# Layernorm statistics moved to an earlier stage, and a residual added by VectorE from PSUM

## The chip, the cores and the metric

The kernel runs on one core of a Trainium2 chip. The time is the device time of one execution in microseconds (us). Engine names are those of the profile: PE is TensorE, PEld its weight load, DVE is VectorE, ACT is ScalarE, POOL is GpSimd, SP is SyncE.

## The reference

x has shape (2, 4096, 256) in fp32. Three layers follow each other, a feed-forward, a memory and a feed-forward once more, each on the layernorm of what is there:

```python
x = x + 0.5 * ffn(layernorm(x))
x = x + memory_layer(layernorm(x))
x = x + 0.5 * ffn(layernorm(x))

def ffn(x):                      # token shift, then a gated square of relu
    x_prev = x shifted by one token
    xr = mu_r * x + (1 - mu_r) * x_prev
    xk = mu_k * x + (1 - mu_k) * x_prev
    return sigmoid(xr @ W_r.T) * (square(relu(xk @ W_k.T)) @ W_v.T)

def memory_layer(x):             # 64 quaternions per token
    keys = x @ Wk.T + bk;  keys = keys / max(norm(keys), 1e-12)
    values = x @ Wv.T + bv
    memory = cumsum(quat_mul(values, keys), axis=1)
    retrieved = quat_mul(memory, quat_conj(keys)) / sqrt(positions)
    return x + (layernorm(retrieved) * ln_g + ln_b) @ Wo.T + bo
```

So the memory stage needs the layernorm of two things: of its input x, and of what was retrieved. Its output is x + n + (...), where n is the layernorm of x, and x + n is the residual.

## The kernel before

The whole of x stays in SBUF, in the tile res. Batch b has NT = 32 tiles of 128 tokens by 256 columns. A feed-forward stage takes CT = 4 tiles in a step, so it has 16 steps (j from 0 to 7, b from 0 to 1). The memory stage takes 2 tiles in a step, so it has 32 steps, numbered s = 2j + b. Each engine has its program written out by hand. Within a step the order of the instructions on an engine is fixed, engines wait for each other by counting semaphores, and an engine also waits by semaphore for its own results. The helper rounds() (L38) runs a body for the first steps, then in a loop, then for the last ones, and has(b, d) tells the body whether the step d places away exists. at(j, b, d) (L52) names that step. Below, (j, b) is such a step.

**A feed-forward step (L362 to L478 on DVE, L1050 to L1119 on PE).** PE makes the transposes of the normalized input (L1062), the keys and the receptance (L1046, three passes of a split product), and the values (L1079). DVE multiplies the values by the gate (gating, L409), forms the difference to the token before (L386), mixes keys and receptance (L394) and squares the keys (L402), and then takes the statistics of a block that is normalized later (stats_of: bn_stats L372, a memset L421, bn_aggr L378). POOL adds the gated values to res (residual, L953) and makes the low parts (L284, L946). ACT copies, applies relu and sigmoid, and normalizes (L704).

**A memory step on DVE (body, L604), in this order:** key_unit writes khat from the keys in PSUM (L561); two bn_stats on res for the step three places ahead (L490); bind (L567, tile xn) and retrieve (L567, tile gating_buffers) form products with khat; two bn_stats on ret, the retrieved tile of the step before (L499); bind of the second tile; four bn_aggr, two for res and two for ret (L515); the halves and the total of the sum of ret (ret_halves and ret_total, L222), with n_var (L524) between them; n_rstd (L530); key_max (L548, tile knorm); retrieve of the second tile; n_gain (L537) and n_shift (L538); key_inverse (L554, tile kinv). One chain of layernorm instructions so serves two layernorms: columns 2 and 3 of the n_ tiles are for res, columns 0 and 1 for ret.

**The other engines in a memory step.** PE (L1202): sum_upto (L1155), sum_after (L1162), transposes (L1129), ret_transposes (L1171), project_keys and project_values (L1135, L1137) and, for the step two places back, output (L1182). ACT (L844): ret_normalize (L812), evict_xT (L793), evict_nT (L825), store_x for the step three places back (L819), add_normalized (L785), key_square (L799), the square root std (L768), key_norm (L805) and normalize for the step three ahead (L776), which waits for n_shift. POOL (L994): ret_sum of the second tile, bind_sum (tiles bhalf and kact), key_sum (tile ksum).

**The residual in the memory stage.** add_normalized turns res into x + n in place. Then output adds that to the product in PSUM by a matmul with the identity matrix, and ACT's store_x copies the sum from PSUM to res. output of a step waits until the store of the step before has emptied the bank (x_done).

```python
                        nc.tensor.matmul(o_bank[:, i, :], ones[:, :], bias3[:, 2 * D:], start=False, stop=False)
                        last = nc.tensor.matmul(o_bank[:, i, :], ident[:, :], t[:, i, :], start=False, stop=True)
```

**The seams.** Between the first feed-forward stage and the memory stage DVE runs first_layernorms(0, 1), the last gating, first_layernorms(1, 3) and first_bind (L654 to L657), and ACT runs first_keys (L827). POOL's last residual of the stage follows the last gating. At the end, first_mix of the second feed-forward stage takes the last layernorm of ret between the two mixes of its keys and those of its receptance (L665). The receptance of that stage uses the PSUM bank of the memory's output, so PE waits there for the last store (L1108).

## Time and profile before

| | |
|---|---|
| median of 3 runs | 753.93 us (753.83 to 755.64) |
| the profiled execution | 753.64 us |
| its span, first to last instruction | 751.9 us |
| mean granted TensorE clock | 0.983 |
| busy: PE, DVE, ACT, POOL | 656.5, 611.3, 418.0, 569.6 us |

In the rows below, a line of a timeline gives the start in us from the beginning of the span, the duration in us, the engine, the line of the kernel, the operation, the output and inputs with their shapes, and how many such instructions were merged (x4). In brackets stands how long the engine was idle before it and what ended that. Two instructions that follow each other on DVE overlap by some 0.1 us, so the distance of their starts tells what one adds. A line of stretches gives for each engine the busy time in the stretch and in parentheses the number of instructions, and then the granted clock of TensorE (1.00 is 2.4 GHz), the share of the DMA engines and the GB/s.

### The profile page before, as it was taken

What the parts mean: (1) busy time and instruction counts of PE and PEld (TensorE: products, weight loads), DVE (VectorE), ACT (ScalarE), POOL (GpSimd) and SP (SyncE); (2) the same over time, 40 slices, a digit from 0 to 9 for tenths busy, and PEclk for the clock granted to TensorE, in tenths of its full rate; (3) what the DMA queues carried; (4) which work ended last, traced back from release to release, by engine and by line L of the source; (5) the groups of instructions that cost most, each with busy time, mean ns of one, the idle gap of its engine ahead of it and who ended that gap; (6) DMA issues with size and microseconds to landing.
All of it is one profiled execution on the core that took longest, in us unless ns stands there. A gap on an engine that the chain in (4) does not pass through costs nothing. (4 is left out here: it accounts for less than half of the span.)

```text
span 751.9 us, 13029 instructions
## 1 busy us (share of the span) xinstructions
PE 656.5 (87%) x3536; PEld 542.1 (72%) x3536; DVE 611.3 (81%) x1378; ACT 418.0 (56%) x743; POOL 569.6 (76%) x879
## 2 busy tenths in 40 slices
PE   2888988999779989988988998898867988988897
PEld 2777878888656667766766676676646878878786
DVE  5868667755679999999999999999976668667744
ACT  4666666664534544554455455445446676666652
POOL 3777778776378888888888888888853877788764
PEclk9999999999988999999999999999979999999999
DMA  7710000000000000000000000000000011011102
GB/s 246 231 57 0 0 0 0 0 1 1 0 0 1 1 0 0 0 0 0 0 0 0 0 0 0 0 0 1 1 1 0 29 57 56 30 54 56 56 29 85
DMA packets 18442, 18.67 MB, mean 25 GB/s; under 512 B 752, under 2 KB 18160, under 8 KB 18416
## 3 DMA queue, kind: packets, MB, share of 16 engines
q1 hardware_dynamic: 18416, 18.36, 7.5%
q8 instruction: 12, 0.20, 0.1%
q14 instruction: 14, 0.11, 0.0%
HBM read 9.97 MB, written 8.39 MB: 24 GB/s over the span
## 5 line engine op out<-in xcount | busy, mean ns | idle before, releaser
L222 POOL TENSOR_TENSOR bhalf<-xn 128x128 f32<-128x128 f32 x256 | 118.3, 493 | 30.4 <-DVE xn L567 30.4
L1135 PE MATMUL bank<-wkv,m_xnT 128*128 128x256 f32 x512 | 135.5, 395 | 5.3 <-DVE khat L561 3.3
L409 DVE TENSOR_TENSOR gating_buffers<-bank,gating_buffers 128x1024 f32<-128x1024 f32 x31 | 38.0, 1225 | 95.8 <-issue 55.0
L1079 PE MATMUL bank<-wffn,kact 128*128 128x256 f32 x512 | 115.8, 379 | 0.0
L1135 PEld LDWEIGHTS bank<-wkv,m_xnT 128*128 128x128 f32 x512 | 92.5, 196 | 25.1 <-issue 4.6
L953 POOL TENSOR_TENSOR res<-res,gating_buffers 128x1024 f32 (+1 forms) x31 | 75.2, 2426 | 39.1 <-DVE gating_buffers L409 39.1
L1079 PEld LDWEIGHTS bank<-wffn,kact 128*128 128x128 f32 x512 | 94.8, 190 | 11.6
L284 POOL TENSOR_TENSOR xk_lo<-xk,xk_hi 128x1024 fp32r<-128x1024 f32 x30 | 71.2, 2372 | 33.4 <-ACT xk_hi L712 33.4
L946 POOL TENSOR_TENSOR xr_lo<-xr,xr_hi 128x1024 fp32r<-128x1024 f32 x32 | 76.0, 2374 | 19.0 <-ACT xr_hi L718 16.8
L567 DVE TENSOR_TENSOR xn<-bank,khat 128x1024 f32<-128x1024 f32 x64 | 77.8, 1216 | 1.4
L567 DVE TENSOR_TENSOR gating_buffers<-bank,khat 128x1024 f32<-128x1024 f32 x64 | 77.6, 1212 | 0.0
L1062 PE MATMUL bank<-ident,xn 128*128 128x128 f32 x256 | 37.2, 292 | 42.3 <-DVE xr L394 30.0
L1046 PE MATMUL bank<-wffn_hi,xr_hi 128*128 128x256 f32 x256 | 71.0, 278 | 0.3 <-ACT res L819 0.3
L724 ACT ACTIVATE relu_k<-bank 128x512 f32<-128x512 f32 x64 | 38.2, 599 | 59.3 <-PE bank L1046 59.3
L1046 PE MATMUL bank<-wffn_hi,xr_lo 128*128 128x256 f32 x256 | 70.9, 277 | 0.0
L1046 PE MATMUL bank<-wffn_lo,xr_hi 128*128 128x256 f32 x256 | 70.8, 277 | 0.0
L222 POOL TENSOR_TENSOR rhalf<-gating_buffers 128x64 f32<-128x64 f32 (+2 forms) x160 | 58.9, 402 | 14.0 <-DVE gating_buffers L567 14.0
L704 ACT ACTIVATE xn<-res,shift,rstd 128x256 f32 (+1 forms) x128 | 66.5, 592 | 5.3 <-POOL shift L941 5.3
L1183 PE MATMUL bank<-wo,normedT 128*128 128x256 f32 x256 | 67.3, 386 | 1.5 <-ACT normedT L825 1.5
L768 ACT ACTIVATE n_std<-n_var 128x4 f32<-128x4 f32 (+1 forms) x36 | 7.4, 205 | 106.4 <-DVE n_var L524 106.3
L1062 PEld LDWEIGHTS bank<-ident,xn 128*128 128x128 f32 x256 | 29.6, 148 | 48.7 <-DVE xr L394 23.4
L776 ACT ACTIVATE m_xn<-res,n_shift,n_rstd 128x256 f32 (+1 forms) x64 | 34.9, 592 | 50.2 <-DVE n_shift L538 50.2
(108 smaller groups left out, 1691.7 us busy)
## 6 DMA issues: line engine op xcount, KB each, us to landing
res<-x SPq DMA_DIRECT2D x16, 512.0 KB, 4.5
out<-res SPq DMA_DIRECT2D x15, 512.0 KB, 2.9
wkv<-w_kv SPq DMA_DIRECT2D x1, 512.0 KB, 8.0
out<-res SPq DMA_DIRECT2D x2, 256.0 KB, 2.1
wffn<-w_k SPq DMA_DIRECT2D x1, 256.0 KB, 3.8
wffn<-w_r SPq DMA_DIRECT2D x1, 256.0 KB, 4.6
wffn<-w_v SPq DMA_DIRECT2D x1, 256.0 KB, 6.0
wo<-w_o SPq DMA_DIRECT2D x1, 256.0 KB, 7.2
```

Of the source, the lines that this page charges most:

```text
L222: last = engine.tensor_tensor(o, a, b, op)
L284: ops.tensor_tensor(xk_lo[:, :, :], xk[:, :, :], xk_hi[:, :, :].bitcast(F32), ALU.subtract).then_inc(e["xklo_done"], 1)
L567: nc.vector.tensor_tensor(dst[:, i, :, :].rearrange("p (a b) n -> p a b n", a=4), of.rearrange("p (a n) -> p a n", n=Q).unsqueeze(2).to_br ...
L704: last = nc.scalar.activation(xn[:, b, i, :], t[:, i, :], ACT.Identity, bias=shift[:, b, i:i + 1], scale=rstd[:, b, i:i + 1])
L724: nc.scalar.activation(relu_k[:, o, :], k_ps[:, o, :], ACT.Relu).then_inc(e["relu_done"], 1)
L946: nc.gpsimd.tensor_tensor(xr_lo[:, :, :], xr[:, :, :], xr_hi[:, :, :].bitcast(F32), ALU.subtract).then_inc(e["xrlo_done"], 1)
L953: nc.gpsimd.tensor_tensor(t, t, gated, ALU.add).then_inc(e["res_done"], 1)
L1046: last = nc.tensor.matmul(out_ap, w(f), v(f), start=k == 0, stop=k == n - 1)
L1062: last = nc.tensor.transpose(xT_ps[:, f, i * P:(i + 1) * P], xn[:, b, i, f * P:(f + 1) * P], ident[:, :])
L1079: last = nc.tensor.matmul(dst[:, i, :], x[:, f, i * P:(i + 1) * P], wffn[:, w, f, :], start=f == 0, stop=f == FC - 1)
L1135: nc.tensor.matmul(dst[:, i, :], m_xnT[:, f, i * P:(i + 1) * P], wkv[:, f, col:col + D], start=f == 0, stop=False)
L1183: nc.tensor.matmul(o_bank[:, i, :], normedT[:, f, i * P:(i + 1) * P], wo[:, f, :], start=f == 0, stop=False)
```

## The change

Two things are changed.

First, the statistics of the memory's input are no longer taken in the memory stage. A new function memory_stats runs at the end of each step of the first feed-forward stage on DVE, on the block whose residual was added last. It waits for that residual, takes four bn_stats, waits for them and writes a memset, takes four bn_aggr, waits for them and copies the eight results into x_moments, a tile that holds the moments of all 64 tiles. Square root, reciprocal, gain and shift are then computed for many tiles at once: for 28 of the 32 tiles of each batch with x_variance(0), x_std_of(0) and x_scales(0), and for the last four with x_variance(1), x_std_of(1) and x_scales(1). DVE runs x_scales(0) after the last gating and x_scales(1) after first_bind. normalize and add_normalized on ACT read x_shift, x_rstd and x_gain, and normalize doesn't wait for scales in each step any more. The chain in the memory stage keeps the two columns for ret, and own_stats gets a memset.

Second, the identity matmul in output and its wait for res_done go away. store_x moves from ACT to DVE, where it adds the PSUM bank to res. It stands between ret_total and n_rstd in the step three places later. At the end, two of the stores stand in last_layernorm and one in last_store, behind first_mix.

```diff
+                def memory_stats(j, b):
+                    s = 2 * j + b
+                    dve.wait_ge(e["res_done"], s + 1)
+                    t = tiles(b * NT + j * CT, CT)
+                    for i in range(CT):
+                        last = nc.vector.bn_stats(x_st[:, i, :], t[:, i, :])
+                    last.then_inc(m["x_st_done"], 1)
+                    dve.wait_ge(m["x_st_done"], s + 1)
+                    nc.vector.memset(spare[:, :], 0.0)
+                    for i in range(CT):
+                        last = nc.vector.bn_aggr(x_mv[:, i, :], x_st[:, i, :])
+                    last.then_inc(m["x_mv_done"], 1)
+                    dve.wait_ge(m["x_mv_done"], s + 1)
+                    nc.vector.tensor_copy(x_moments[:, b, bass.ds(j * CT, CT), :], x_mv[:, :, :]).then_inc(m["x_moments_done"], 1)
...
                         if has(b, 4):
                             stats_of(j + 2, b)
+                        if stage == 0 and has(b, -1):
+                            memory_stats(*at(j, b, -1))
...
+                def x_variance(n, first, end):
+                    dve.wait_ge(m["x_moments_done"], 2 * (end // CT))
+                    nc.vector.tensor_scalar(x_var[:, :, first:end], x_moments[:, :, first:end, 1], LN_EPS, None,
+                                            ALU.add).then_inc(m["x_var_done"], 1)
+                def x_scales(n, first, end):
+                    dve.wait_ge(m["x_std_done"], n + 1)
+                    nc.vector.reciprocal(x_rstd[:, :, first:end], x_std[:, :, first:end]).then_inc(m["x_rstd_done"], 1)
+                    dve.wait_ge(m["x_rstd_done"], n + 1)
+                    nc.vector.tensor_scalar(x_gain[:, :, first:end], x_rstd[:, :, first:end], 1.0, None, ALU.add)
+                    nc.vector.scalar_tensor_tensor(x_shift[:, :, first:end], x_moments[:, :, first:end, 0], -1.0,
+                                                   x_rstd[:, :, first:end], ALU.mult, ALU.mult).then_inc(m["x_scales_done"], 1)
...
+                def store_x(j, b):
+                    s = 2 * j + b
+                    dve.wait_ge(m["O_done"], s + 1)
+                    dve.wait_ge(m["res_done"], s + 1)
+                    t = tiles(b * NT + j * 2, 2)
+                    nc.vector.tensor_tensor(t, o_bank, t, ALU.add).then_inc(m["x_done"], 1)
...
                 def body(j, has, start_last):
                     for b in range(2):
-                        s = 2 * j + b
+                        behind = has(b, -1)
                         if not has(b, 1):
                             start_last()
-                        where = at(j, b, -1) if has(b, -1) else None, at(j, b, 3) if has(b, 3) else None
                         if has(b, 1):
                             key_unit(*at(j, b, 1))
-                        ln_stats_res(s + 3, *where)
-                        if has(b, 1):
                             bind(*at(j, b, 1), 0)
                         retrieve(j, b, 0)
-                        ln_stats_ret(s + 3, *where)
-                        own_stats(s + 3, *where)
+                        if behind:
+                            ln_stats(*at(j, b, -1))
                         if has(b, 1):
                             bind(*at(j, b, 1), 1)
-                        ln_moments(s + 3, *where)
+                        if behind:
+                            own_stats(*at(j, b, -1))
+                            ln_moments(*at(j, b, -1))
                         ret_halves(nc.vector, j, b, 0)
-                        ln_variance(s + 3, *where)
+                        if behind:
+                            ln_variance(*at(j, b, -1))
                         ret_total(nc.vector, j, b, 0)
-                        ln_inverse(s + 3, *where)
+                        if has(b, -3):
+                            store_x(*at(j, b, -3))
+                        if behind:
+                            ln_inverse(*at(j, b, -1))
...
             ffn_steps()
-            first_layernorms(0, 1)
+            x_variance(0, 0, NT - CT)
             last_gating()
-            first_layernorms(1, 3)
+            x_scales(0, 0, NT - CT)
+            memory_stats(NJ - 1, 1)
+            x_variance(1, NT - CT, NT)
             first_bind()
+            x_scales(1, NT - CT, NT)
...
                 def first_keys():
                     load_table(ACT.Sqrt)
-                    std(0, 0, 2, 4)
+                    x_std_of(0, 0, NT - CT)
+                    act.wait_ge(m["x_scales_done"], 1)
                     normalize(0, 0)
...
                         if behind:
                             evict_nT(j - 1, b)
-                        if has(b, -3):
-                            store_x(*at(j, b, -3))
...
                     pe.wait_ge(m["normedT_done"], s + 1)
-                    pe.wait_ge(m["res_done"], s + 1)
-                    t = tiles(b * NT + j * 2, 2)
                     need(pe, m["x_done"], s)
...
-                        nc.tensor.matmul(o_bank[:, i, :], ones[:, :], bias3[:, 2 * D:], start=False, stop=False)
-                        last = nc.tensor.matmul(o_bank[:, i, :], ident[:, :], t[:, i, :], start=False, stop=True)
+                        last = nc.tensor.matmul(o_bank[:, i, :], ones[:, :], bias3[:, 2 * D:], start=False, stop=True)
```

## Rows read from the trace of the kernel before

**Rows 1.** The page's first part, busy us, share and instructions of each engine.
```profile
PE 656.5 (87%) x3536; PEld 542.1 (72%) x3536; DVE 611.3 (81%) x1378; ACT 418.0 (56%) x743; POOL 569.6 (76%) x879
```
**Rows 2.** Stretches: memory steps 0 to 2, then 3 to 29; PE, PEld, DVE, ACT, POOL.
```profile
213.75:246.46 32.71, 26.79 (x116) 19.27 (x114) 31.52 (x71) 12.45 (x27) 26.39 (x59) 0.90 0.00 1
246.46:540.12 293.66, 267.49 (x1350) 206.14 (x1350) 289.99 (x670) 150.60 (x325) 250.02 (x541) 1.00 0.00 0
```
**Rows 3.** Timeline of DVE in one steady memory step.
```profile
409.99 0.69 DVE L561 TENSOR_TENSOR khat<-bank,kinv 128x512 f32<-128x512 f32 x1
410.60 0.74 DVE L490 BATCH_NORM_STATS2 n_st<-res 128x6 f32 x2
411.25 1.21 DVE L567 TENSOR_TENSOR xn<-bank,khat 128x1024 f32<-128x1024 f32 x1
...
415.43 0.37 DVE L515 BATCH_NORM_AGGREGATE n_mv<-n_st 128x2 f32<-128x6 f32 x4
415.71 1.88 DVE L222 TENSOR_TENSOR rhalf<-gating_buffers 128x64 f32<-128x64 f32 x5
...
418.22 0.18 DVE L530 RECIPROCAL n_rstd<-n_std 128x4 f32<-128x4 f32 x1
...
419.74 0.15 DVE L537 TENSOR_SCALAR n_gain<-n_rstd 128x2 f32<-128x2 f32 x1
419.80 0.15 DVE L538 SCALAR_TENSOR_TENSOR n_shift<-n_mv,n_rstd 128x4 f32<-128x4 f32 x1
419.87 0.94 DVE L554 RECIPROCAL kinv<-knorm 128x128 f32<-128x128 f32 x1
```
**Rows 4.** Timeline of DVE in one step of the first feed-forward stage.
```profile
95.63 1.40 DVE L372 BATCH_NORM_STATS2 st<-res 128x6 f32 x4
...
100.41 1.22 DVE L409 TENSOR_TENSOR gating_buffers<-bank,gating_buffers 128x1024 f32<-128x1024 f32 x1 [2.96 <-issue]
```
**Rows 5.** Timeline of several engines from the first seam to memory step 0.
```profile
191.62 0.16 DVE L524 TENSOR_TENSOR n_var<-n_mv,eps 128x2 f32<-128x2 f32 x1
...
195.19 1.09 ACT L776 ACTIVATE m_xn<-res,n_shift,n_rstd 128x256 f32<-128x256 f32 x2 [0.50 <-DVE n_shift L538]
...
196.43 0.63 PE L1129 MATMUL bank<-ident,m_xn 128*128 128x128 f32 x4 [0.95 <-ACT m_xn L776]
...
196.88 2.35 POOL L953 TENSOR_TENSOR res<-res,gating_buffers 128x1024 f32<-128x1024 f32 x1 [6.52 <-DVE gating_buffers L409]
...
197.77 1.47 DVE L524 TENSOR_TENSOR n_var<-n_mv,eps 128x2 f32<-128x2 f32 x1
...
203.52 0.23 DVE L548 TENSOR_SCALAR knorm<-knorm 128x128 f32<-128x128 f32 x1 [1.74 <-ACT knorm L805]
...
205.61 2.04 PE L1135 MATMUL bank<-wkv,m_xnT 128*128 128x256 f32 x4 [3.27 <-DVE khat L561]
...
212.13 0.55 DVE L548 TENSOR_SCALAR knorm<-knorm 128x128 f32<-128x128 f32 x1 [4.28 <-ACT knorm L805]
...
222.22 0.23 DVE L548 TENSOR_SCALAR knorm<-knorm 128x128 f32<-128x128 f32 x1 [0.29 <-ACT knorm L805]
```
**Rows 6.** Timeline of DVE at the second seam, its two differences.
```profile
560.83 1.23 DVE L386 TENSOR_TENSOR diff<-bank,xnT 128x1024 f32<-128x1024 f32 x1 [3.70 <-ACT xnT L695]
...
574.76 1.23 DVE L386 TENSOR_TENSOR diff<-bank,xnT 128x1024 f32<-128x1024 f32 x1 [3.61 <-ACT xnT L695]
```
**Rows 7.** Timeline of DVE in step 30, where no bn_stats on res follow khat.
```profile
540.12 0.69 DVE L561 TENSOR_TENSOR khat<-bank,kinv 128x512 f32<-128x512 f32 x1
540.85 1.22 DVE L567 TENSOR_TENSOR xn<-bank,khat 128x1024 f32<-128x1024 f32 x1
```
**Rows 8.** Timeline of PE in a steady step, output.
```profile
405.73 1.03 PE L1183 MATMUL bank<-wo,normedT 128*128 128x256 f32 x4
...
406.70 0.60 PE L1186 MATMUL bank<-res,ident 128*128 x2
407.14 1.03 PE L1183 MATMUL bank<-wo,normedT 128*128 128x256 f32 x4
```

More of the change, by code:

```diff
@@ L476, in last_blocks @@
                         nc.vector.tensor_tensor(t, t, gated[:, span, :], ALU.add).then_inc(last_done, 1)
-                return stats_of, first_mix, steps, last_gating, last_blocks
+                return stats_of, memory_stats, first_mix, steps, last_gating, last_blocks
             def mem():
-                def ln_stats_res(r, ret_at, res_at):
-                    if res_at is not None:
-                        jj, q = res_at
-                        need(dve, m["res_done"], capped(r - 1))
-                        t = tiles(q * NT + jj * 2, 2)
-                        for i in range(2):
-                            nc.vector.bn_stats(n_st[:, q, 2 + i, :], t[:, i, :]).then_inc(m["st_done"], 1)
@@ new lines, in ln_stats, with ln_moments @@
+                def ln_stats(j, b):
+                    s = 2 * j + b
+                    need(dve, m["normed_done"], s - 1)
+                    for i in range(2):
+                        dve.wait_ge(ret_done[i], s + 1)
+                        nc.vector.bn_stats(n_st[:, b, i, :], ret[:, b, i, :]).then_inc(m["st_done"], 1)
+                def ln_moments(j, b):
+                    s = 2 * j + b
+                    for i in range(2):
+                        last = nc.vector.bn_aggr(n_mv[:, b, i, :], n_st[:, b, i, :])
+                    last.then_inc(m["mv_done"], 1)
@@ L584, in retrieve @@
                     all_products(rprod, b, i, memory[b], rprod_done[i])
-                def first_layernorms(start, end):
-                    dve.wait_ge(ffn_sems[0]["res_done"], B)
-                    for r in range(start, end):
-                        where = None, (r // 2, r % 2)
-                        ln_stats_res(r, *where)
-                        own_stats(r, *where)
-                        ln_all(r, *where)
                 def first_bind():
@@ L627, in body @@
                         retrieve(j, b, 1)
-                        ln_scales(s + 3, *where)
+                        if behind:
+                            ln_scales(*at(j, b, -1))
                         if has(b, 2):
@@ L775, in normalize @@
                     for i in range(2):
-                        last = nc.scalar.activation(m_xn[:, i, :], t[:, i, :], ACT.Identity, bias=n_shift[:, b, 2 + i:3 + i],
-                                                    scale=n_rstd[:, b, 2 + i:3 + i])
+                        last = nc.scalar.activation(m_xn[:, i, :], t[:, i, :], ACT.Identity, bias=x_shift[:, b, bass.ds(j * 2 + i, 1)],
+                                                    scale=x_rstd[:, b, bass.ds(j * 2 + i, 1)])
                     last.then_inc(m["xn_done"], 1)
@@ L784, in add_normalized @@
                     for i in range(2):
-                        last = nc.scalar.activation(t[:, i, :], t[:, i, :], ACT.Identity, bias=n_shift[:, b, 2 + i:3 + i],
-                                                    scale=n_gain[:, b, i:i + 1])
+                        last = nc.scalar.activation(t[:, i, :], t[:, i, :], ACT.Identity, bias=x_shift[:, b, bass.ds(j * 2 + i, 1)],
+                                                    scale=x_gain[:, b, bass.ds(j * 2 + i, 1)])
                     last.then_inc(m["res_done"], 1)
@@ L857, in body @@
                             key_square(j + 1, b)
[L858 removed]
+                        if has(b, -1):
+                            std(*at(j, b, -1))
                         if ahead:
```

136 lines of the change are left out of this document (58 added, 78 removed).

## The prediction

> **What bounds the kernel now.** I read the page first: its busy line names no single bound, PE 87%, DVE 81%, POOL 76% [rows 1]. So I split the span by stage. In the memory stage, from 246.46 to 540.12 us, DVE is busy for 289.99 of 293.66 us, while PE has 267.49, POOL 250.02 and ACT 150.60 [rows 2]: VectorE sets the pace, and a change there is worth its effect on DVE's list of instructions. That stretch holds 27 steps, so a step takes 10.88 us. One step in DVE's timeline [rows 3] begins with khat at 409.99 and ends with kinv at 419.87 + 0.94, with nothing idle. In the first feed-forward stage it is different: DVE sits idle for 2.96 us before each gating [rows 4], because PE still makes the values. What is added there lies beside other work as long as it stays under 2.96 us. Last I read the two seams, where a chain runs through ACT, PE, POOL and DVE in turn [rows 5, 6].
>
> The profiled execution took 753.64 us (span 751.9 and 1.7 around it), the median of the runs is 753.93. I work from 753.64 and take the result as the median; the two differ by 0.04%. Under 0.3%, some 2.3 us, a difference here can't be told from no change.
>
> **The part in the first feed-forward stage.** Per step memory_stats adds four bn_stats, a memset, four bn_aggr and one copy of 8 columns. The same list without the copy is there now: from 95.63 to 97.45 (where the idle time before gating begins, 100.41 - 2.96), 1.82 us [rows 4]. With some 0.2 us for the copy and its wait (the small tensor-scalar operations take 0.15 [rows 3]) that is 2.0 us, from 97.45 to 99.45. The gating comes at 100.41, so 0.9 us is left: cost nothing. If the cover were gone, each 0.1 us over it would cost 1.5 us in 15 steps. The wait for the residual's sum holds nothing, since POOL has finished the block of the step before long since.
>
> **The part in the steady memory step.** Spacings count, not durations, since neighbours overlap.
> - Out goes the pair of bn_stats on res. Now khat to bn_stats to bind takes 411.25 - 409.99 = 1.26 us [rows 3]. But the pair also covered bind's wait for khat's own completion; near the end of the stage, where no such pair runs, khat to bind takes 540.85 - 540.12 = 0.73 [rows 7]. Gain 0.53, not 0.65.
> - Two of four bn_aggr: 415.71 - 415.43 = 0.28 for four [rows 3], so 0.14. n_gain: 419.80 - 419.74 = 0.06 [rows 3].
> - In comes the memset, under 0.07 us (bounds 0 and 0.1; the four bn_aggr are 0.07 each).
> - In comes store_x, 512 columns from PSUM and SBUF. The nearest row is khat, the same size and the same two memories: spacing 410.60 - 409.99 = 0.61, busy 0.69 [rows 3]. Bounds 0.55 and 0.75; I take 0.61.
> - Sum: -0.53 - 0.14 - 0.06 + 0.07 + 0.61 = -0.05 us. I use -0.06 with the rounding of the rows. VectorE gets as much work as it loses. For the 26 steps 3 to 28: -1.6 us.
>
> At the wait for khat the Trainium skill speaks otherwise. "VectorE: DVE Perf Modes", section "The DRAIN you can't avoid", says that the next operation starts only once the pipe is empty and that a semaphore between two operations costs nothing extra. By that, khat to bind would cost 0.61 with or without a wait, and the sum at the end would be 3.1 us lower. The trace disagrees, 0.61 without one against 0.73 with one.
>
> **What goes beside it.** PE loses two ident matmuls a step, each with 407.14 - 406.70 = 0.44 us up to the next matmul [rows 8], so 0.88 us, and ACT loses a copy of 0.6. Neither bounds a step. But output now waits for DVE's store_x of the step before. Counted from khat, store_x starts at 7.65 and ends at 8.34; output, which starts 6.6 after khat now (405.73 against 409.99 less a step of 10.88) [rows 3, 8], is held to 8.4 and, shorter by 0.88, ends at 10.4. Behind it on PE stands sum_upto, ready at 11.0; retrieve wants it at 10.8 + 1.86 = 12.7. Slack 1.7 us, so the new wait costs nothing. The keys of the next step come 0.4 us later on PE, ksq still is there when POOL comes to it. Without that slack each step would grow by what is missing.
>
> **Steps without the pair or without the store.** Steps 0 to 2 take 32.71 us now, 1.2 of them idle on DVE [rows 2]. They lose the statistics and have no store_x; step 0 has no layernorm of ret any more (n_var, n_rstd and the rest are some 0.9 us), and ACT's normalize, which used to wait for n_shift at the end of a step, is free, so knorm is early. I get 9.3, 10.2 and 10.1 us: -3.1. Steps 29 and 30 have no bn_stats on res now, so they just gain store_x and the memset: +1.4. In step 31 the store lies before DVE's idle 3.70 us [rows 6]: nothing.
>
> **The first seam.** This decides. Now the first layernorm of the memory is finished before the last gating, and ACT normalizes at 195.19 [rows 5]. After the change x_scales stands behind the last gating on DVE, which starts when the values are there, at 195.5, and takes 1.2 as each gating does [rows 4]: from 196.7 on a reciprocal of 56 columns (0.5 us, between n_rstd's 0.18 for 4 and kinv's 0.94 for 128 columns [rows 3]), x_gain, x_shift. And just then POOL runs the last residual, 196.88 to 199.23 [rows 5]. n_var, with two SBUF inputs, started at 197.77 in that stretch and took 1.47 us, to 199.24, against 0.16 at 191.62 with POOL at rest [rows 5]. x_shift also has two SBUF tensor inputs, and x_gain is of knorm's kind, which took 0.55 beside POOL's work at 212.13 and 0.23 with POOL at rest at 203.52 [rows 5]. So I let both wait for POOL: scales at 199.5, normalize at 199.55, 4.35 later. Bounds: 197.6 if they aren't held, 199.7 if both are in full.
>
> The Trainium skill has the rule behind this: "SBUF — State Buffer", section "Who interferes with whom", says that DVE and GpSimd share a port pair as an exclusive lock, taken by tensor-scalar operations in the two-port mode and, against a GpSimd operation that reads SBUF, by any DVE operation with two SBUF inputs; the second to issue blocks fully. The row of n_var agrees.
>
> Then PE: it ended its values at 195.48 (0.95 before 196.43) [rows 5] and would idle until 200.8, 5.3 us. After an idle time of 3.27 us it now comes back at half clock: four matmuls take 2.04 us at 205.61 [rows 5] against 1.03 for the four of output in the steady step [rows 8]. So transposes (1.1), eviction (0.6) and keys (4.2) run at 1.2 GHz and the values in part; ACT's order puts evict_xT(0,1) before key_norm, so knorm is there at 210.4 and key_max(0,0) at 210.5, not 203.52: +7.0 us (bounds +2.4 and +8). From there to khat(0,1) the chain is as now, half clock included, but for x_scales(1) before the loop: +0.5.
>
> **The second seam.** PE has three outputs there without ident matmuls, -0.9 each, but each store on DVE adds 0.6 to the chain between key mix and receptance mix. PE's transposes(0,1) come at 570.4, and DVE, after the last store at 570.4 and the moved stats_of, is at its difference at 572.95 where it is at 574.76 now [rows 6]: -1.8 us (bounds -0.8 and -2.8).
>
> **Sum.** 7.0 + 0.5 - 3.1 - 1.6 + 1.4 - 1.8 = +2.4 us, 753.6 + 2.4 = 756.0 us. Its own range is 754.0 to 758.5.
>
> **The rivals.**
> - The steady step grows instead of shrinking by 0.05. The place is key_max, which moves 0.6 us later, from the end of POOL's bhalf into its sums for kact. There it can meet a POOL instruction; held ones took 0.55 against 0.23 [rows 5]. From +0.1 us a step on it decides the sign clearly; at +0.25 a step, 26 steps give +6.5: 756.0 + 1.6 + 6.5, about 764; at 0.1, 760. Against it: key_max at 222.22 stood at the start of such sums and took 0.23 [rows 5]. Chance 0.18.
> - The clock holds at keys(0,1). PE idles 3.1 us before it by my count, against the 3.27 us that preceded the fall at 205.61 [rows 5]. Then 4 keys and bias passes take 2.1 us less: 753.9. Chance 0.17.
> - The residual doesn't hold the scales (x_gain slips in ahead, x_shift isn't blocked as n_var was). Normalize comes at 197.65, 1.9 earlier: 754.1; if the shorter idle keeps PE at full clock too, 2.6 more: 751.5. For it: nothing shows x_shift's kind of operation beside a long POOL instruction. Chance 0.13.
> - A wait for the engine's own result costs nothing here: khat to bind then takes 0.61, each of 26 steps 0.12 less, 3.1 us in all: 752.9. The row of 0.73 [rows 7] speaks against it. Chance 0.05. (The Trainium skill's page on VectorE, named above, has this as its rule.)
> - The change doesn't do what it says: the moved statistics don't leave the bound engine. They do; but the eviction comes to it in their place, which is the forecast itself. The rest, 0.05, is for a memory step that shrinks more than I see (key_max finding POOL at rest, -0.2 a step: 751).
>
> **How the numbers follow.** The forecast has 0.42. Half of its own range lies above 756.2, where slower begins. Slower: 0.21 + 0.18 + 0.01 = 0.40. Faster (under 751.7): the low end of the third rival 0.05, some of the fourth 0.02, the rest 0.05 = 0.12. Same: 0.48. The range reaches from 751.0 to 763.0, so that about 1 in 10 is left out on each side.
>
> **What would show it.** In the first stage gating keeps its spacing of 11.0 us. In the memory stage khat to khat is 10.8 us, DVE still without idle time, khat to bind 0.73, PE idle before output. At the first seam ACT's first m_xn begins near 199.5 right after POOL's residual, PE's first keys take 2 us per four matmuls, key_max(0,0) begins near 210.5. Step 0 is near 9.3 us. If m_xn begins at 197.7, or key_max before 207, the time is lower; if the steady step is over 10.9, or key_max takes 0.4 in it, it is higher.

## The result, and the profile after

The changed kernel takes 759.07 us (median of 5 runs, 758.83 to 760.51) beside 755.64 for the kernel before in the same runs (753.83 to 755.79). The ratio is 1.006, with a 95% interval of 1.0043 to 1.0077: slower by some 4.5 us, where I forecast slower by 2.4. The medians alone lie only 3.4 us apart, since the times of the kernel before fall into two groups (753.83 and 753.93, then 755.64 to 755.79) and its median lies in the upper one. It was timed a second time, with e10_after_again below, and gave 1.0058 (1.0045 to 1.0072). The profiled executions differ by 5.2 us (753.64 and 758.83; spans 751.9 and 757.1), and their difference can be followed row by row.

The first part of the page of the changed kernel: busy us, share, instructions. Against [rows 1] PE lost 23 us and ACT 14, DVE gained 31: PE and ACT were relieved, but the engine that sets the memory stage's pace was not.

```profile
span 757.1 us, 12708 instructions
PE 633.6 (84%) x3408; PEld 527.9 (70%) x3408; DVE 642.7 (85%) x1437; ACT 403.9 (53%) x709; POOL 568.6 (75%) x879
```

The first feed-forward stage: DVE in a step from the middle, then POOL and DVE ahead of the last gating but one. The memory's statistics fit in the middle of the stage: 0.92 us of idle time is left before gating, where I had counted 0.9. Towards the end they don't. The copy of 8 columns takes 0.17 us at 99.74 and 1.79 at 186.16, where it ends together with POOL's xr_lo (185.55 + 2.38 = 187.93).

```profile
99.74 0.17 DVE L444 COPY x_moments<-x_mv 128x8 f32 x1 [0.17 <-DVE x_mv L441]
100.83 1.23 DVE L411 TENSOR_TENSOR gating_buffers<-bank,gating_buffers 128x1024 f32<-128x1024 f32 x1 [0.92 <-PE bank L1086]
...
185.55 2.38 POOL L953 TENSOR_TENSOR xr_lo<-xr,xr_hi 128x1024 fp32r<-128x1024 f32 x1
...
186.16 1.79 DVE L444 COPY x_moments<-x_mv 128x8 f32<-128x8 f32 x1
187.87 1.21 DVE L411 TENSOR_TENSOR gating_buffers<-bank,gating_buffers 128x1024 f32<-128x1024 f32 x1
```

The last line has no idle time before it: this gating was held by the copy. The last gating of the stage comes at 196.65, 1.08 after the 195.57 of before.

The first seam of the changed kernel, several engines (start, duration, and in brackets the idle time and what ended it), against [rows 5]:

```profile
196.65 1.23 DVE L411 TENSOR_TENSOR gating_buffers<-bank,gating_buffers 128x1024 f32<-128x1024 f32 x1 [2.93 <-issue]
197.79 0.49 DVE L509 RECIPROCAL x_rstd<-x_std 128x56 f32<-128x56 f32 x1
197.95 2.34 POOL L960 TENSOR_TENSOR res<-res,gating_buffers 128x1024 f32<-128x1024 f32 x1 [6.39 <-DVE gating_buffers L411]
198.31 2.06 DVE L511 TENSOR_SCALAR x_gain<-x_rstd 128x56 f32<-128x56 f32 x1
...
200.25 0.20 DVE L512 SCALAR_TENSOR_TENSOR x_shift<-x_moments,x_rstd 128x56 f32<-128x56 f32 x1
...
200.50 1.09 ACT L794 ACTIVATE m_xn<-res,x_shift,x_rstd 128x256 f32<-128x256 f32 x2 [5.08 <-DVE x_shift L512]
...
201.73 1.09 PE L1136 MATMUL bank<-ident,m_xn 128*128 128x128 f32 x4 [5.58 <-ACT m_xn L794]
...
203.49 2.08 PE L1142 MATMUL bank<-wkv,m_xnT 128*128 128x256 f32 x4 [0.68 <-ACT m_xnT L811]
...
210.38 0.23 DVE L550 TENSOR_SCALAR knorm<-knorm 128x128 f32<-128x128 f32 x1 [7.78 <-ACT knorm L823]
```

All of the chain that I had drawn is there: the scales behind the last gating, x_gain held until POOL's residual is done (197.95 + 2.34 = 200.29), normalize right after, PE back at half clock (2.08 us for four key matmuls), key_max(0,0) at 210.38.

One steady memory step on DVE, against [rows 3], and PE's output in it, against [rows 8]:

```profile
402.88 0.69 DVE L563 TENSOR_TENSOR khat<-bank,kinv 128x512 f32<-128x512 f32 x1
403.61 1.22 DVE L569 TENSOR_TENSOR xn<-bank,khat 128x1024 f32<-128x1024 f32 x1
...
407.67 0.18 DVE L526 BATCH_NORM_AGGREGATE n_mv<-n_st 128x2 f32<-128x6 f32 x1
...
407.83 2.25 DVE L225 TENSOR_TENSOR rhalf<-gating_buffers 128x64 f32<-128x64 f32 x5
410.00 0.42 DVE L531 TENSOR_TENSOR n_var<-n_mv,eps_pos 128x2 f32<-128x2 f32 x1
410.35 0.41 DVE L225 TENSOR_TENSOR ret<-rhalf 128x256 f32<-128x256 f32 x1
410.68 0.68 DVE L603 TENSOR_TENSOR res<-bank,res 128x512 f32 x1
411.28 0.15 DVE L536 RECIPROCAL n_rstd<-n_std 128x2 f32<-128x2 f32 x1
411.35 0.20 DVE L550 TENSOR_SCALAR knorm<-knorm 128x128 f32<-128x128 f32 x1
```
```profile
411.50 1.10 PE L1188 MATMUL bank<-wo,normedT 128*128 128x256 f32 x4 [1.67 <-DVE res L603]
```

The stages of the changed kernel (window, its length, busy us and instructions of PE, PEld, DVE, ACT, POOL, granted clock): memory steps 0 to 2, steps 3 to 29, then to the first difference of the second feed-forward, to the second, and to the next gating. The first two answer [rows 2].

```profile
220.42:251.04 30.62, 25.59 (x110) 18.74 (x110) 28.94 (x57) 13.23 (x28) 25.53 (x58) 0.89 0.00 1
251.04:543.83 292.79, 241.07 (x1238) 189.31 (x1236) 288.82 (x594) 138.14 (x296) 250.07 (x541) 1.00 0.00 0
543.83:565.71 21.88, 13.09 (x47) 9.76 (x46) 18.01 (x56) 7.01 (x15) 15.35 (x36) 0.75 0.00 0
565.71:578.09 12.38, 10.67 (x52) 8.01 (x51) 10.15 (x27) 7.84 (x13) 2.38 (x1) 0.90 0.01 1
578.09:591.48 13.39, 10.33 (x56) 9.21 (x55) 8.47 (x27) 10.07 (x17) 9.26 (x14) 0.87 0.00 1
```

Before, the last three are 20.71, 13.93 and 11.76 us long. With those landmarks the 5.2 us are split up without a rest:

| Stretch | Forecast | Measured, from rows |
|---|---|---|
| start to key_max(0,0) | +7.0 | +6.86 (203.52, 210.38) |
| to khat(0,1) | +0.5 | -0.19 (213.75, 220.42 stand 6.67 apart) |
| steps 0 to 2 | -3.1 | -2.09 (32.71, 30.62) |
| 26 steady steps | -1.6 | -1.45 (283.46, 282.01) |
| steps 29, 30, to the first difference | +1.4 | +1.75 (30.91, 32.66) |
| between the two differences | -1.8 | -1.55 (13.93, 12.38) |
| to the next gating, and the rest | 0 | +1.63 (11.76, 13.39) and +0.24 |
| sum | +2.4 | +5.2 |

### The profile page after: what moved, and what is told of

Same layout as the page of the kernel before. It is cut to its first block and busy times, and to the rows that moved or that the text cites. A ratio compares the mean times of both kernels' runs of the same rounds, so it can differ in the third digit from the quotient of the medians.

```text
span 757.1 us, 12708 instructions
## 1 busy us (share of the span) xinstructions
PE 633.6 (84%) x3408; PEld 527.9 (70%) x3408; DVE 642.7 (85%) x1437; ACT 403.9 (53%) x709; POOL 568.6 (75%) x879
## 5 line engine op out<-in xcount | busy, mean ns | idle before, releaser
L1188 PE MATMUL bank<-wo,normedT 128*128 128x256 f32 x256 | 70.1, 405 | 50.8 <-DVE res L603 49.5
L1188 PEld LDWEIGHTS bank<-wo,normedT 128*128 128x128 f32 x256 | 45.6, 199 | 69.4 <-issue 60.1
L225 DVE TENSOR_TENSOR rhalf<-gating_buffers 128x64 f32<-128x64 f32 (+2 forms) x160 | 69.2, 494 | 0.0
```

The lines of the kernel that those rows point to most:

```text
L225: last = engine.tensor_tensor(o, a, b, op)
L1188: nc.tensor.matmul(o_bank[:, i, :], normedT[:, f, i * P:(i + 1) * P], wo[:, f, :], start=f == 0, stop=False)
```

## The experiments

Four questions were open. Is the cost really in the first seam, and the two parts worth what I said (e1 to e4)? Why do the halves of ret take longer in the steady step than before (e5)? What holds x_gain, and what do the waits at output cost (e6, e7)? Is it the clock that makes the first keys late (e8, e9, e11)?

Since medians taken at different times differ a little, I compare ratios to the kernel before, and rows by their distance from a landmark. The one that shifts most is the start: in the profiles of e1, e5, e6, e8, e9, e10 and e11 everything from some 35 us on comes 1.4 to 2.1 us later, since PE's granted clock dropped between some 29 and 35 us. The last section has its numbers.

**e1_scales_first**: the changed kernel, x_scales(0) ahead of the last gating.

```diff
-            last_gating()
             x_scales(0, 0, NT - CT)
+            last_gating()
```

> The changed kernel with one edit: x_scales(0) stands ahead of the last gating on DVE instead of behind it. My theory: in the changed kernel DVE's first m_xn release comes at 200.5 us, since x_scales(0) waits behind the last gating and then behind POOL's last residual (x_gain took 2.06 us, to 200.3). Ahead of the gating the square root is there at 195.4, reciprocal 0.5, gain and shift 0.3, so m_xn begins near 196.4 and the gating is late by 0.1 at most. PE's idle time before its first transposes falls from 5.6 us to about 1.5, so they and the first keys run at full clock, and key_max(0,0) moves from 210.4 back to about 205. The time falls by 5 us against the changed kernel, to about that of the kernel before (ratio 0.999). Rival: the seam is bound elsewhere (the statistics of the last block, or the chain of knorm), then key_max(0,0) stays within 1 us of 210.4 and the ratio near 1.006.

Measured: 753.65 us, ratio 0.9981 (0.9966 to 0.9996). The loss is gone, and a little more. In its timeline x_gain takes 0.19 us, since POOL is not at work yet:

```profile
197.55 0.19 DVE L511 TENSOR_SCALAR x_gain<-x_rstd 128x56 f32<-128x56 f32 x1
...
197.81 1.23 DVE L411 TENSOR_TENSOR gating_buffers<-bank,gating_buffers 128x1024 f32<-128x1024 f32 x1
197.90 1.09 ACT L794 ACTIVATE m_xn<-res,x_shift,x_rstd 128x256 f32<-128x256 f32 x2 [0.92 <-DVE x_shift L512]
...
199.14 0.63 PE L1136 MATMUL bank<-ident,m_xn 128*128 128x128 f32 x4 [1.42 <-ACT m_xn L794]
...
207.59 0.23 DVE L550 TENSOR_SCALAR knorm<-knorm 128x128 f32<-128x128 f32 x1 [3.86 <-ACT knorm L823]
```

This profile has the late start (1.60 at the gating of 100.83, which is at 102.43 here), so key_max(0,0) is 4.4 us earlier than in the changed kernel. I had expected the first keys to run at full clock, and that didn't come about: after 1.42 us of idle time they are at half clock too (1.89 us for a group of four), and from the transposes to key_max it still takes 8.45 us (8.65 in the changed kernel). What the moved line gives is the earlier m_xn.

**e2_stats_only**: the changed kernel, with the residual left to TensorE and ScalarE as before. **e3_store_only**: the kernel before, with the residual added by VectorE and nothing else.

The heart of the diff of e2 against the changed kernel (e3 has the same edit the other way round, against the kernel before); store_x also goes back to ACT's program and out of DVE's:

```diff
-                    nc.vector.tensor_tensor(t, o_bank, t, ALU.add).then_inc(m["x_done"], 1)
+                    nc.scalar.copy(tiles(b * NT + j * 2, 2), o_bank).then_inc(m["x_done"], 1)
...
-                        last = nc.tensor.matmul(o_bank[:, i, :], ones[:, :], bias3[:, 2 * D:], start=False, stop=True)
+                        nc.tensor.matmul(o_bank[:, i, :], ones[:, :], bias3[:, 2 * D:], start=False, stop=False)
+                        last = nc.tensor.matmul(o_bank[:, i, :], ident[:, :], t[:, i, :], start=False, stop=True)
```

> The changed kernel with its second part undone: the statistics are taken in the first feed-forward stage as in the change, but the residual is added by the identity matmul on PE and copied out by ACT, as before. My theory: the steady memory step is DVE's list, 10.78 us in the changed kernel, and store_x is 0.60 of it; the step falls to about 10.18 us, 26 steps give 15.6 us, and the time is near 742 us (ratio 0.984). Rival: PE or POOL becomes the bound once DVE's list is shorter (PE had about 9.6 us of work a step with the identity matmul, POOL 9.3): then the step stays over 10.5 us, DVE shows idle time in it, and the time is over 750.

> The kernel before with only the second part of the change: store_x on DVE adds PSUM to res, the identity matmuls are gone, the statistics stay in the memory stage. My theory: store_x adds 0.60 us to each of 29 steady steps, 10.88 to 11.48 us, 17 us in all, less 1.5 at the second seam: near 770 us (ratio 1.021). The first seam is that of the kernel before, key_max(0,0) near 203.5. Rival: taking 0.88 us from PE and 0.6 from ACT gives something back in the step: then the step is 11.2 or less.

Measured: e2 743.21 us, ratio 0.9855 (0.9828 to 0.9881), steady step 10.313 us (250.82 to 518.97 for 26). e3 764.44 us, ratio 1.0133 (1.0115 to 1.0152), steady step 11.241. Against the 10.902 of before the statistics are worth -0.59 and the store costs +0.34 a step; both together give not -0.25 but -0.055 (10.847). So the one part is a clear gain and the other a clear loss, and in the changed kernel they nearly cancel. For e2 I had expected 742 us, for e3 770: the store costs less than its own 0.60 us.

My list had -0.66 for the first and +0.61 for the second. In e3 the store costs only 0.34. Most of what is missing is this: n_rstd and key_max stand behind it and no longer wait, they are followed by the next instruction after 0.08 and 0.12 us there, after 0.20 and 0.18 before. And in e3 PE's wait for the store does something that I had excluded; its output falls to half clock inside steady steps:

```profile
412.60 1.10 PE L1183 MATMUL bank<-wo,normedT 128*128 128x256 f32 x4 [2.15 <-DVE res L609]
...
413.70 1.92 PE L1183 MATMUL bank<-wo,normedT 128*128 128x256 f32 x4
```

**e4_stats_scales_first**: e2 and e1 together.

> Both edits together: statistics in the first feed-forward stage, the residual on PE and ACT as before, and x_scales(0) ahead of the last gating. If the two are independent, it is 5 us under the kernel with the statistics alone, near 737 us (ratio 0.977). If the seam's loss is hidden by something else once the steps are shorter, it is equal to it.

Measured: 738.88 us, ratio 0.9792 (0.9773 to 0.9811). It beats the kernel before by some 16 us and the changed one by some 20. The steady step is 10.317 us as in e2, key_max(0,0) comes at 206.13.

**e5_extra_aggr**: the changed kernel, with work added to the bound engine.

```diff
+                        nc.vector.bn_aggr(x_mv[:, i, :], n_st[:, b, i, :])
                         last = nc.vector.bn_aggr(n_mv[:, b, i, :], n_st[:, b, i, :])
```

> The changed kernel with two more bn_aggr on VectorE in every memory step, ahead of the operation that halves the retrieval's result; their result is not used. They add about 0.14 us of work to each of some 30 steps. Theory A (VectorE waits at the halving for GpSimd's key_sum, whose end sets the time at which the halving ends): the halving starts later and takes that much less, 2.03 us from start to start where the changed kernel has 2.17; the steady step stays at 10.85 us and the kernel within 1 us of the changed kernel. Rival B (VectorE's list is simply a sum): the halving stays at 2.17, the step is 10.99 us and the kernel 4 us longer than the changed kernel, 763 us.

Measured: 760.55 us, ratio 1.0088 (1.007 to 1.0106); by the times alone, neither theory is excluded. The trace decides for A in the steady step. The step is 10.852 us for 10.847, and from the last gating to the one at the second seam it is 394.40 us (198.27 to 592.67), in e10_after_again 394.39. In its timeline the halves begin 5.08 us after khat, where the changed kernel has 4.95, and n_var follows 7.12 us after khat in both:

```profile
404.42 0.69 DVE L564 TENSOR_TENSOR khat<-bank,kinv 128x512 f32<-128x512 f32 x1
...
409.50 2.12 DVE L225 TENSOR_TENSOR rhalf<-gating_buffers 128x64 f32<-128x64 f32 x5
411.54 0.42 DVE L532 TENSOR_TENSOR n_var<-n_mv,eps_pos 128x2 f32<-128x2 f32 x1
```
```profile
409.27 0.72 POOL L990 TENSOR_TENSOR ksum<-ksq 128x256 f32<-128x256 f32 x1
```

POOL's key_sum begins 4.85 us after khat in both (407.73 in the changed kernel), and n_var follows its start by 2.27 us in both. So the end of the halves goes with POOL's key_sum, and 0.13 us more of DVE's work ahead of them costs nothing. The kernel before has the same distance, 2.28 us, though DVE comes to its halves 0.47 us after the start of key_sum and not 0.10 as in the changed kernel:

```profile
415.24 0.73 POOL L982 TENSOR_TENSOR ksum<-ksq 128x256 f32<-128x256 f32 x1
417.52 0.43 DVE L524 TENSOR_TENSOR n_var<-n_mv,eps 128x4 f32<-128x4 f32 x1
```

**e6_residual_dve**: the changed kernel, the last residual of the first feed-forward on VectorE behind x_scales(0), not on POOL.

```diff
             x_scales(0, 0, NT - CT)
+            dve.wait_ge(ffn_sems[0]["gated_done"], NS)
+            last_t = tiles(2 * NT - CT, CT)
+            nc.vector.tensor_tensor(last_t, last_t, gated, ALU.add).then_inc(ffn_sems[0]["res_done"], 1)
...
                     rounds(pool, NJ, 1, 2, body)
-                    if stage == 0:
-                        residual(NJ - 1, 1)
```

> The changed kernel with the last residual addition of FFN0 on VectorE behind x_scales(0), where the changed kernel has it on GpSimd. Theory A (x_gain is held by GpSimd's residual at the shared SBUF port): x_gain takes about 0.2 us, where the changed kernel has 2.06; the first normalized x of the memory (m_xn) starts at about 198.7 us where the changed kernel has 200.5; key_max(0,0) starts some 1.8 us earlier, at about 208.6, if the clock behaves alike, and the kernel is 1 to 2 us faster than the changed kernel. The residual on VectorE lies in the time in which it waits for keys(0,0). Rival B (x_gain is long for another reason, the distance to its own inputs): x_gain stays near 2 us and the first seam and the time don't change.

Measured: 756.67 us, ratio 1.0028 (1.0016 to 1.0041), some 2.3 us under the changed kernel. x_gain takes 0.19 us, and m_xn starts 2.02 us after the last gating (200.24 - 198.22) where it is 3.85 in the changed kernel: the 1.8 us that I had put down to POOL's residual.

```profile
199.89 0.19 DVE L511 TENSOR_SCALAR x_gain<-x_rstd 128x56 f32<-128x56 f32 x1
...
200.12 1.22 DVE L671 TENSOR_TENSOR res<-res,gating_buffers 128x1024 f32<-128x1024 f32 x1
200.24 1.09 ACT L797 ACTIVATE m_xn<-res,x_shift,x_rstd 128x256 f32<-128x256 f32 x2 [3.24 <-DVE x_shift L512]
```

Only 0.76 of it arrives at key_max(0,0) (12.97 after the last gating, 13.73 in the changed kernel), since more of the keys run at half clock in this profile (2.08, 1.92 and 1.75 us for a group of four matmuls; in the changed kernel 2.08, 1.45 and 1.03). Against e10_after_again, where they take 2.08, 1.92 and 1.74, it is 2.0 (14.97 - 12.97).

**e7_early_store**: the changed kernel, store_x ahead of the first retrieve of the step.

```diff
                             bind(*at(j, b, 1), 0)
+                        if has(b, -3):
+                            store_x(*at(j, b, -3))
                         retrieve(j, b, 0)
...
                         ret_total(nc.vector, j, b, 0)
-                        if has(b, -3):
-                            store_x(*at(j, b, -3))
```

> The changed kernel with store_x ahead of the retrieval's first operation of the step, where the changed kernel has it after. Theory A (in the changed kernel store_x covers the waits of n_rstd and knorm for VectorE's own results, and TensorE's wait for PSUM at the output costs nothing): TensorE's idle time ahead of the output falls from 1.67 us to under 0.3, but the steady step grows by 0.1 to 0.2 us, to 10.95 to 11.05, and the kernel by 3 to 5 us over the changed kernel; in the second seam the half clock at the last output goes, worth 0.6 us of that. Rival B (the wait at the output costs): the step is shorter than 10.85 us and the kernel faster than the changed kernel.

Measured: 758.31 us, ratio 1.0054 (1.0035 to 1.0073), not to be told from the changed kernel. The trace shows neither theory as written. PE's output has no idle time before it any more, and the steady step is 0.07 us shorter (10.776), not 0.1 to 0.2 longer. It is not the wait at output: n_rstd and key_max do wait again (spaced 0.20 and 0.14), but the halves, which DVE reaches 5.55 us after khat, take 1.92 us for 2.17. As in e5, they are shorter when they begin later; only here they begin 0.84 us after the start of key_sum, and n_var follows it by 2.76 us, no longer by 2.27. Steps 28 and 29 are 0.24 us longer each, its first seam is longer (15.29 us from the last gating to key_max(0,0), 13.73 in the changed kernel, with three groups of keys at half clock), and a half-clock stretch in the second seam is missing, in this one profile: the second difference to the next gating takes 11.72 us, as before, where it is 13.39 in the changed kernel. I can't say what share of its 10 runs has that.

**e8_pe_filler** and **e9_filler_short**: the changed kernel, with 22 and with 11 matmuls without use while PE waits for the memory's first m_xn. Nothing else differs.

```diff
+                pe.wait_ge(ffn_sems[0]["gate_done"], NS)
+                for _ in range(22):
+                    nc.tensor.matmul(o_bank[:, 0, :], wkv[:, 0, 0:P], wkv[:, 0, 0:D], start=True, stop=True)
```

> The changed kernel with 22 matmuls without use on TensorE between the last values of FFN0 and the first transposes of the memory, into a bank that is overwritten later. They keep TensorE at work where the changed kernel has it idle for some 5 us. Theory A (the granted clock falls to half in that idle time and makes keys(0,0) and keys(0,1) slow, 2.08 us where 1.04 is the time at full clock): the keys run at full clock, key_max(0,0) starts 2 to 3 us earlier than 210.4 us, and the kernel is 1 to 3 us faster than the changed kernel. Rival B (what follows m_xn on ScalarE and VectorE sets the time of key_max(0,0), not the clock): key_max(0,0) stays within 0.5 us of 210.4 and the time doesn't change.

> As e8_pe_filler, with 11 matmuls in place of 22, since those ran for 9.66 us and held the first transposes back by some 3.6 us. The 11 should take 4.8 us and end ahead of the first transposes, which stay 5.1 us behind the last gating. Theory A (the half clock after TensorE's idle time is what makes the first keys late): from the first transposes to key_max(0,0) it is 6.8 us, as in e8_pe_filler, where the changed kernel has 8.65; key_max(0,0) starts 11.9 us after the last gating where the changed kernel has 13.7, and the kernel is 1.9 us faster or more. Rival B (the clock falls all the same, since these matmuls do not count or end too early): 8.6 us or more from the transposes to key_max(0,0), and no gain.

Measured: e8 759.84 us, ratio 1.0074 (1.0058 to 1.0089): no gain. Its filler ran for 9.66 us, longer than the idle time, and held the transposes back to 206.88, 4.98 us behind m_xn instead of 1.23. But the clock behaved as theory A says: 6.74 us from the transposes to key_max(0,0). In e9 the filler fits, and the time follows: 756.35 us, ratio 1.0025 (1.0005 to 1.0045), 2.5 us under e10_after_again. The filler there ends at 202.94, ahead of the transposes at 203.70. The timeline of e9:

```profile
198.03 4.91 PE L1198 MATMUL bank<-wkv 128*128 128x256 f32 x22
...
203.70 0.66 PE L1136 MATMUL bank<-ident,m_xn 128*128 128x128 f32 x4 [0.75 <-ACT m_xn L794]
...
205.03 1.13 PE L1142 MATMUL bank<-wkv,m_xnT 128*128 128x256 f32 x4 [0.68 <-ACT m_xnT L811]
...
210.49 0.23 DVE L550 TENSOR_SCALAR knorm<-knorm 128x128 f32<-128x128 f32 x1 [5.83 <-ACT knorm L823]
...
212.58 2.05 PE L1142 MATMUL bank<-wkv,m_xnT 128*128 128x256 f32 x4 [2.95 <-DVE khat L563]
```

From the transposes to key_max(0,0) it is 6.79 us for 8.65 (9.89 in e10), and 11.80 from the last gating for 13.73 (14.97 in e10). The last line shows what is given back: the half clock now comes at keys(0,1), after 2.95 us of idle time, and khat(0,0) to khat(0,1) takes 9.55 us where it is 8.79 in the changed kernel. It isn't the 2.95 us alone that brings this: e8 has the same idle time there, and its keys(0,1) take 1.10 us.

**e10_after_again**: the changed kernel itself, beside e9 and e11.

> The changed kernel itself, on the same chip and beside the same runs of the kernel before as e9_filler_short and e11_best_filler, to compare them with it directly. The first comparison gave a ratio of 1.006; both theories expect 1.005 to 1.008 here.

Measured: 759.43 us, ratio 1.0058 (1.0045 to 1.0072). Its profile shows how far one execution of the same kernel is from another: from m_xn (201.87) to key_max(0,0) (213.00) it takes 11.13 us, where the first profile has 9.88, since three groups of keys and not two run at less than full clock.

**e11_best_filler**: e4_stats_scales_first with three such matmuls (range(3)).

> e4_stats_scales_first (the statistics moved, the residual left to TensorE and ScalarE, x_scales(0) ahead of the last gating) with three matmuls without use on TensorE ahead of the memory's first transposes. In e4_stats_scales_first TensorE is idle there for 1.42 us, and the first keys run at half clock; from the transposes to key_max(0,0) it is 8.45 us. Theory A (even this short idle time lets the clock fall): with 1.3 us of it filled the clock holds, it is 6.8 us, and the kernel is 1 to 1.7 us faster than e4_stats_scales_first, some 737 us. Rival B (the clock falls for what lies before, not for this idle time): it stays at 8.4 us and the time at 739 us.

Measured: 738.89 us, ratio 0.9787 (0.9774 to 0.98). The mechanism is A's, the time B's. From the transposes (199.01) to key_max(0,0) (205.81) it is 6.80 us for 8.45: with the idle time of 1.42 us filled, the keys behind it run at full clock. But the next keys are at half clock again (2.04 at 207.90), which takes 0.5 us back, and no gain can be measured in the end. In these two profiles 1.25 us of it is there at khat(0,1) (18.24 us behind the last gating for 19.49), and 0.45 is left at the gating behind the second seam (373.79 for 374.24), where the values take 4.90 us in e11 and 3.62 in e4.

```profile
197.51 1.46 PE L1198 MATMUL bank<-wkv 128*128 128x256 f32 x6
...
199.01 0.66 PE L1133 MATMUL bank<-ident,m_xn 128*128 128x128 f32 x4
...
205.81 0.23 DVE L550 TENSOR_SCALAR knorm<-knorm 128x128 f32<-128x128 f32 x1 [1.58 <-ACT knorm L808]
...
207.90 2.04 PE L1139 MATMUL bank<-wkv,m_xnT 128*128 128x256 f32 x4 [2.95 <-DVE khat L563]
```

## Why the prediction was right, and where its sizes were off

The direction and the place were right: the memory stage gives a little back, and the first seam takes more. e1 shows the place; one line moved there is worth 0.8%. The size was too small, 2.4 us for 4.5, and the 759.07 us lie just over the forecast's own range (754.0 to 758.5). That is near where rival one begins (760), but the steady step didn't grow: what was missing is in steps 0 to 2 and behind the second difference, and that the sum came out no further off owes something to errors that cancel.

**First feed-forward, predicted 0, measured +1.08.** The cover was sized rightly (0.92 us left for 0.9), but from a step in the middle of the stage. Some 0.4 of it is there from the first steps on (gating at 34.61 for 34.20, at 100.83 for 100.41). The rest is from the last steps, where the order of the list brings the copy beside POOL's xr_lo, 1.8 us for 0.2: the distance to the kernel before is 0.43 at the gating of 178.09, 1.26 at the next and 1.08 at the last. I used the port rule for the scales and not for the copy, which is in the same change. The Trainium skill names copy among the operations that can take the shared pair ("SBUF — State Buffer", "Who interferes with whom"); the 1.79 agrees. That no copy would cost less wasn't tried.

**The hold of the scales, right.** Normalize was predicted at 199.55, 4.35 later; less the 1.08 it came at 199.42. It was x_gain that POOL held, and e6 confirms the cause. Rival three falls.

**The half clock, right in kind; its size isn't the same in every execution.** From normalize to key_max(0,0) I had 10.95 us. In this profile it took 9.88: I let nearly all keys run at half speed, and the clock was back at some 206. In e10_after_again, the same kernel, it took 11.13. e9 shows that it is the clock: with PE kept at work it is 7.94 us (202.55 to 210.49). So the forecast of 210.5 was met at 210.38 by luck: the stage before ended 1.1 us late, and the half clock of this execution was 1.1 us shorter than mine.

The +6.86 at this seam are 1.08 for the late end of the stage, 1.83 for the hold (m_xn 3.85 us after the last gating, 2.02 in e6), 2.40 for scales that stand behind the gating at all (2.02 after it, where m_xn was 0.38 ahead of it before), and 1.94 for the clock (9.88 for the 7.94 of e9), less 0.39, since at full clock that way took 8.33 before.

**Rival two, the clock holds at keys(0,1): half true, and priced too high.** Its groups take 1.30, 1.92, 1.50 and 1.03 us in the changed kernel and 1.10, 1.03, 1.03 and 1.03 in e10; in the kernel before they take 2.04, 1.91, 1.91 and 1.11. But khat(0,0) to khat(0,1), 8.98 us before (204.77 to 213.75), is 8.79 and 8.46: it gives some 0.5 us, not 2.1. The 0.19 are the whole difference of the table's second line, where I had +0.5.

**Steps 0 to 2, predicted -3.1, measured -2.09.** Step 0 takes 9.87 us for 9.3; key_max waits 1.41 us for ACT in step 1. I summed DVE's list where the chain through the other engines still set the end.

**The steady step, predicted -0.06, measured -0.055, and not as listed.** khat to bind is 0.73 as said, so rival four falls: an own wait costs 0.12 us here. The store takes 0.60. But two entries were missing, and they nearly cancel, which is luck: store_x covers the waits of n_rstd and key_max (0.07 and 0.12 for 0.20 and 0.18), and the halves take 2.17 for 1.81. Their end is tied to the start of POOL's key_sum in both kernels, and that moved up by only 0.40 us (4.85 after khat for 5.25), where DVE's list ahead of them lost 0.77 (4.95 for 5.72). e2 and e3 show the parts, -0.59 and +0.34, and that they don't add up; e5 shows why. Rival one didn't come about at key_max (0.20 us), but something of its kind did, at the halves. What remains of the last rival, a step that shrinks by 0.2, is in neither profile of the changed kernel.

**PE's wait at output, predicted free, is free in the steady step.** It is 1.67 us, and e7, which takes it away, gains 0.07 us, no more than the halves give. At the end of the stage it isn't: PE is idle for 4.01 us before the output at 552.11, falls to half clock, and DVE waits 0.59 us for it at 557.25. That is in the +1.75 for 1.4.

**The second seam, predicted -1.8, measured -1.55; behind it +1.63 that I had not.** There the transposes of the second feed-forward and the values behind them run at half clock in part, 1.85 and 4.55 us; at full clock (e7) they take 1.06 and 3.62:

```profile
585.18 1.85 PE L1069 MATMUL bank<-ident,xn 128*128 128x128 f32 x8 [3.06 <-DVE xr L396]
...
586.82 4.55 PE L1086 MATMUL bank<-wffn,kact 128*128 128x256 f32 x16
```

This is the step of the prediction that failed outright: it ended at the difference, and let all behind it be as before. PE was idle for 2.12 us before those transposes and is for 3.06 now, since it gets through the products ahead of them sooner: it starts them 1.85 us ahead of the difference instead of 1.33, and no longer waits 0.33 us for ACT's copy in them. From the second difference to the next gating it is over 13 us in seven profiles with that gap (after, e1, e5, e6, e8, e9, e10), and 11.75 in e2 and e4, whose gap is 2.02. But e7 has the gap of 3.06 and 11.72, e3 one of 3.20 and 11.72, and e11 has 2.03 and 13.44. So the gap doesn't decide alone. Whether the change brings the half clock there or only some executions have it is open, and of the kernel before there is one profile; I made no experiment there.

## What to carry to other kernels

Work that leaves the bound engine is worth only what isn't put in its place: here the moved statistics gave 11 us and the residual cost 10, and leaving the second part out made 743 us of 759. When work moves across a stage boundary, read the boundary's list in order and ask of each small operation which long instruction of another engine it will stand beside; one line moved ahead of the gating was worth 5 us. And sum a list only between the points where another engine sets the time: ahead of such a point 0.13 us more cost nothing (e5), and of 0.77 us that went 0.40 arrived.

## What the runs showed of the hardware that I had not expected

- The granted clock falls in some executions and not in others of the same kernel. In the first feed-forward it was 1.00 between 30 and 40 us in the changed kernel's first profile, and 0.72 between 30 and 35 in e10_after_again's, of the same kernel, which made all behind it 1.4 us later (last gating at 198.03 for 196.65). What decides wasn't looked for.
- An idle time of PE of no more than 1.42 us, ahead of four short transposes, was followed by half clock on the keys (e1, e4: 1.89 and 1.96 us for four matmuls); with three matmuls in it they took 1.13 (e11), and so they did before, after an idle time of 0.95. Filling it took the half clock from these keys and gave it to the next. The length of an idle time doesn't decide alone: after the same 2.95 us keys(0,1) take 2.05 in e9 and 1.10 in e8 and e10.
- An operation of a few columns is held by POOL about as long as a larger one: the copy of 8 columns took 1.79 us for 0.17, x_gain with 56 columns 2.06 for 0.19.
- Beside POOL's key_sum the end of DVE's halves stands 2.27 us behind the start of key_sum, whether they begin 0.10, 0.23 or 0.47 us behind it (changed kernel, e5, before).
